# Mixture-of-experts routing by a gathered token list, with one shared-expert step after the expert tiles, in an eight-layer kernel on one core

## The reference, cut to what matters

```
def _L2_ffn_ref(x, router_w, expert_bias, w1, w3, w2, sw1, sw3, sw2):
    E, NSH, TOPK = (8, 2, 2)                      # HID = 256
    def _ffn(x, w1, w2, w3):
        return jax.nn.silu(x @ w1.T) * (x @ w3.T) @ w2.T
    xf = x.reshape(-1, d)                          # the normalised x
    shared = jnp.zeros_like(xf)
    for i in range(sw1.shape[0]):                  # two shared experts, every token
        shared = shared + _ffn(xf, sw1[i], sw2[i], sw3[i])
    logits = xf @ router_w.T + expert_bias
    rw, sel = jax.lax.top_k(logits, TOPK)          # each token's two best of 8 experts
    rw = jax.nn.softmax(rw, axis=-1)
    combine = jnp.einsum('tk,tke->te', rw, jax.nn.one_hot(sel, E))
    # out = sum over the 8 experts of combine[:, e] * _ffn(xf, w1[e], w2[e], w3[e])
    return out + shared
x = x + _L2_ffn_ref(_layernorm(x, axis=-1), ...)
x = x + _L3_xattn_ref(_layernorm(x, axis=-1), ctx_768, ...)
```

## Time and profile before

| | |
|---|---|
| median of 3 runs | 541.45 us (539.92 to 545.09) |
| the profiled execution's own time | 537.47 us |
| its span in the profile | 535.3 us, so 2.2 us lie around it |
| busy: PE, DVE, ACT, POOL | 84%, 71%, 51%, 35% |
| L2's mixture of experts in the span | from 359.7 us (first shared product) to 441.6 us (last tile's down product) |

### The profile page before, as it was taken

The page is one execution under the profiler, slowest core; times in us unless marked ns, Lnnn a source line. Parts: engine busy times, 40 slices in busy tenths (PEclk is TensorE's granted clock), DMA queues, the critical chain, the costliest instruction groups (busy, mean ns, idle before and its releaser), DMA issues.

```text
span 535.3 us, 9362 instructions
## 1 busy us (share of the span) xinstructions
PE 451.3 (84%) x3045; PEld 317.5 (59%) x3045; DVE 378.2 (71%) x1371; ACT 271.2 (51%) x854; POOL 189.7 (35%) x220
## 2 busy tenths in 40 slices
PE   3940689999988999999878989999989987777976
PEld 2310689899553567667446546775656653654845
DVE  4799988936766467863696868875744476938776
ACT  2798487620515566653245526652233348547553
POOL 5999994030231900001401553026420515110042
PEclk9755579999999999999999999999999998879999
DMA  7107000000455000000001230000341211000001
GB/s 259 78 1 299 6 2 3 1 1 1 157 222 239 0 3 1 2 1 1 1 12 28 67 85 1 2 1 29 101 118 40 70 45 46 10 1 1 1 0 39
DMA packets 17846, 26.46 MB, mean 49 GB/s; under 512 B 1988, under 2 KB 15236, under 8 KB 17287
## 3 DMA queue, kind: packets, MB, share of 16 engines
q1 hardware_dynamic: 16774, 23.78, 12.9%
q0 software_dynamic: 1024, 2.10, 1.4%
HBM read 21.07 MB, written 6.77 MB: 52 GB/s over the span
## 4 chain that ended last, share of the span: by engine, by line
PE 57%; DVE 19%; POOL 11%; ACT 6%; issue 5%; DMA 1%; SPq 0%; ACTq 0%; DVEq 0%; POOLq 0%
PE bank L1988 4%; PE bank L1054 3%; PE bank L791 3%; PE bank L1100 3%; PE bank L1081 3%; ACT arenaB L2405 3%; PE bank L2003 2%; PE bank L2349 2%; PE bank L2323 2%; PE bank L269 2%; PE bank L705 2%; PE bank L1724 2%; DVE arenaB L439 2%; PE bank L1697 2%; PE bank L262 2%
## 5 line engine op out<-in xcount | busy, mean ns | idle before, releaser
L218 POOL TENSOR_SCALAR rtmp<-mv 128x4 f32<-128x4 f32 x14 | 3.5, 248 | 130.6 <-DVE mv L197 106.4
L269 PE MATMUL bank<-in_ctx 128*128 128x512 f32 (+2 forms) x124 | 38.6, 439 | 0.0
L2405 ACT ACTIVATE arenaB<-bank,arenaB 128x77 f32<-128x77 f32 x88 | 27.2, 353 | 10.8 <-DVE arenaB L2424 10.7
L1988 PE MATMUL bank<-arenaA,in_dft 128*128 x60 | 30.6, 594 | 1.9 <-issue 1.9
L1111 DVE TENSOR_REDUCE nmax<-bank 128x1 f32<-128x512 f32 x32 | 20.5, 684 | 13.2 <-PE bank L1054 13.2
L2323 PE MATMUL bank<-arenaB,xnT 128*128 128x385 f32 (+1 forms) x48 | 22.5, 605 | 7.3 <-ACT arenaB L2405 6.7
L2048 ACT ACTIVATE in_dft<-bank 128x256 f32<-128x256 f32 x30 | 11.5, 384 | 33.7 <-PE bank L1988 33.7
L2215 DVE TENSOR_TENSOR in_ffn<-in_dft,bank 128x256 f32<-128x256 f32 x30 | 12.6, 419 | 22.3 <-ACT in_dft L2048 22.3
L439 DVE MATCH_REPLACE8 arenaB<-arenaB 128x77 f32<-128x77 f32 x128 | 26.8, 223 | 0.0
L269 PEld LDWEIGHTS bank<-in_ctx 128*128 128x128 f32 x124 | 19.4, 191 | 12.3 <-issue 11.7
L276 ACT COPY xnT<-bank 128x512 f32<-128x512 f32 x14 | 8.2, 585 | 34.8 <-PE bank L262 34.8
(11 more groups left out here) (511 smaller groups left out, 1358.8 us busy)
## 6 DMA issues: line engine op xcount, KB each, us to landing
arenaA<-in_moe_dram SPq DMA_DIRECT2D x1, 3840.0 KB, 11.7
in_dft<-in_dft_dram SPq DMA_DIRECT2D x1, 2048.0 KB, 7.5
in_dft<-in_head_dram SPq DMA_DIRECT2D x1, 2048.0 KB, 7.4
arenaA<-in_l_dram SPq DMA_DIRECT2D x1, 2048.0 KB, 16.0
xs_scratch<-in_moe_dram SPq DMA_DIRECT2D x2, 960.0 KB
arenaB<-xs_scratch SPq DMA_DIRECT2D x6, 256.0 KB, 3.4
ys_scratch<-arenaB SPq DMA_DIRECT2D x6, 256.0 KB
vw_scratch<-in_dft SPq DMA_DIRECT2D x32, 38.5 KB
```

The costliest lines, as they stand in the source:

```text
L269: nc.tensor.matmul(bank[into][:, 0:width], ident, packed["ctx"][:, 0:width], start=True, stop=True)
L1988: nc.tensor.matmul(bank[i % 2][:], xsT[:, g % 2, (i - i0) * P:(i - i0 + 1) * P], V["moe"][:, bass.ds(off[i], 2 * HE)], start=True, stop=Tr ...
L2405: ins = nc.scalar.activation(p3[:, n % 3, h, :], bank3(n, i)[:, (h - h0) * NC:(h - h0 + 1) * NC], ACT.Exp, bias=mx3[:, n % 3, h:h + 1], ac ...
```

## The change

Four things are done together.

1. *The list is made on chip the other way round.* `vec_route_slots` also builds, from each token's slot, two sets of 0/1 (or token-number) matrices, and `pe_inverse` multiplies them: 8 matmuls give, for each tile and each place in it, the number of the token that belongs there (0 for padding). DVE copies it to `token` (`vec_tokens`).
2. *Rows are gathered, not scattered.* SP stores the normalised rows in order to `xn_scratch` (256 KB for each batch). POOL issues one indirect gather for each of the 15 tiles from `xn_scratch` straight into `xs` on chip. The scatter, its waits, SP's reloads and the filling of `xs_scratch` near the start are gone. The tile groups become (0,3), (3,7), (7,11), (11,15).
3. *One shared step is moved.* `NSTEP` is 6: step 3 (expert 9, batch 1) leaves the half-steps. Its two up half-steps stand on PE behind tiles 28 and 29 (`i >= NT2`), its down product in `pe_attend3` between `scores(1)` and `scores(2)`, its addition to `X` on DVE at n = 1 of `vec_attend3`.
4. *Orders around it.* Batch 1's scores, places and slots move to n = 4, 4 and 5; `pe_offsets(0)` from n = 7 to n = 4. Batch 0's transposes into L3 and ACT's `warm` now stand behind the moved step.

```
-TILE_GROUPS = [(4 * g, min(4 * g + 4, TILES)) for g in range(-(-TILES // 4))]
+TILE_GROUPS = [(max(4 * g - 1, 0), 4 * g + 3) for g in range(-(-TILES // 4))]
...
-            sp.wait_ge(bias_rows, 48)
-            for b in range(NB):
-                sp.dma_start(A[f"xs_scratch{b}"].rearrange("(p j) d -> p (j d)", p=P), A["moe"][:, 0:TILES * D]).then_inc(bias_rows, 16)
...
-        NSTEP = 2 * len(SHARED)
+        NSTEP = 2 * (len(SHARED) - 1)
...
+        def pe_inverse(pe, b):
+            pe.wait_ge(*past(inverse_ready, b + 1))
+            for g in range(2 * TB):
+                ins = nc.tensor.matmul(bank[6 + b][:, P:P + TILES], at_place[:, g, :], in_tile[:, g, :], start=(g == 0), stop=(g == 2 * TB - 1))
+            ins.then_inc(inverse_mm[0], 1)
...
         def pe_moe(pe):
...
                 if n == 3:
-                    pe_turn(pe, ln_done, NT * 8, xn, [1], TURN8)
+                    pe_inverse(pe, 0)
                 if n == 4:
                     pe_logits(pe, 1)
-                if n == 7:
-                    pe_rank(pe, 1)
+                    off.extend(pe_offsets(pe, 0))
                 if n < NSTEP:
...
+                    pe_shared_up(n)
-                if n == NSTEP - 1:
-                    off.extend(pe_offsets(pe, 0))
+                if n == 3:
+                    pe_turn(pe, ln_done, NT * 8, xn, [1], TURN8)
+                if n == 5:
+                    pe_rank(pe, 1)
                 if n == NSTEP + 1:
                     pe_turn_tiles(pe, 0)
...
         def pe_tiles(pe, off):
...
+                    if i == 0:
+                        pe_inverse(pe, 1)
...
-                if i == NT2:
-                    pe_turn(pe, ln_done, NT * 9, xn, [0], TURN3)
+                if i >= NT2:
+                    pe_shared_up(NSTEP + i - NT2)
+            pe_turn(pe, ln_done, NT * 9, xn, [0], TURN3)
...
         def act_tiles(act):
...
                 if i == NT2:
-                    nc.scalar.activation(warm[:], ident[0:1, 0:1], ACT.Exp)
-                    act_turned(act, 7, which=[0], banks=TURN3)
+                    act_shared(act, NSTEP)
                 if i - 2 in LAST2:
                     act_ys(act, LAST2[i - 2])
+            act_shared(act, NSTEP + 1)
+            nc.scalar.activation(warm[:], ident[0:1, 0:1], ACT.Exp)
+            act_turned(act, 7, which=[0], banks=TURN3)
...
+        def pool_rows(pool, b):
+            pool.wait_ge(*past(token_ready, b + 1))
+            pool.wait_ge(*past(xn_stored[b], 16))
+            for g, (i0, i1) in enumerate(TILE_GROUPS):
+                if b:
+                    pool.wait_ge(xs_in[g], 16 * (i1 - i0))
+                for i in range(i0, i1):
+                    nc.gpsimd.indirect_dma_start(out=xs[:, b * TILES + i, :], out_offset=None, in_=A[f"xn_scratch{b}"],
+                                                 in_offset=bass.IndirectOffsetOnAxis(ap=token[:, b, i:i + 1], axis=0)).then_inc(xs_in[g], 16)
...
         def sync_tiles(sp):
...
+            for b in range(NB):
+                sp.wait_ge(ln_done, NT * 8 + (b + 1) * TB)
+                sp.dma_start(A[f"xn_scratch{b}"].rearrange("(q p) d -> p q d", p=P), xn[:, b * TB:(b + 1) * TB, :]).then_inc(xn_stored[b][0], 16)
...
         def vec_route_slots(dve, st, b):
...
             st.link(Vv.tensor_reduce(slotf, rks, AX.X, ALU.add))
-            Vv.tensor_scalar(slot[:, b, :], slotf, float(P), None, ALU.mult).then_inc(slot_ready[0], 1)
+            st.link(Vv.tensor_scalar(tmag, slotf, -63.5 / P, MAGIC, ALU.add, ALU.add))
+            st.link(Vv.scalar_tensor_tensor(below_tile, tmag, MAGIC, slotf, ALU.subtract, ALU.subtract))
+            if b:
+                dve.wait_ge(*past(inverse_mm, b))
+            Vv.tensor_tensor(at_place, bm(V["place"], 2 * TB), bc(below_tile, P, 2 * TB, P), ALU.is_equal)
+            st.link(Vv.tensor_tensor(in_tile, bm(V["jmag"], 2 * TB), bc(tmag, P, 2 * TB, TILES), ALU.is_equal))
+            Vv.tensor_tensor(in_tile, in_tile, bc(V["token"], P, 2 * TB, TILES), ALU.mult).then_inc(inverse_ready[0], 1)
+            Vv.tensor_scalar(slot[:, b, :], slotf, float(P), None, ALU.mult)
...
+        def vec_tokens(dve, b):
+            dve.wait_ge(*past(inverse_mm, b + 1))
+            nc.vector.tensor_copy(token[:, b, 0:TILES], bank[6 + b][:, P:P + TILES]).then_inc(token_ready[0], 1)
...
         def vec_moe(dve, st):
-            for n in range(NSTEP + 4):
-                if n == NSTEP - 1:
+            for n in range(NSTEP + 3):
+                if n == 4:
+                    vec_route_scores(dve, st, 1)
+                    vec_route_places(dve, st, 1)
+                if n == 5:
                     vec_route_slots(dve, st, 1)
                 if n < NSTEP:
+                    vec_shared(dve, n)
...
                 if n == 0:
                     vec_route_slots(dve, st, 0)
+                if n == 1:
                     vec_normalise(dve, 8, X, xn, [1])
-                if n == 4:
-                    vec_route_scores(dve, st, 1)
-                if n == 5:
-                    vec_route_places(dve, st, 1)
-                if n == 6:
+                    vec_tokens(dve, 0)
+                if n == 3:
                     vec_route_weights(dve, st, 0)
...
         def vec_tiles(dve, st):
...
+                if i == 0:
+                    vec_tokens(dve, 1)
+                if i == 6:
+                    vec_route_weights(dve, st, 1)
...
-                if i == NT2 - 1:
-                    vec_normalise(dve, 9, X, xn, [0])
+            vec_normalise(dve, 9, X, xn, [0])
+            vec_shared(dve, NSTEP)
+            vec_shared(dve, NSTEP + 1)
...
             scores(0)
+            pe.wait_ge(hid_ready, NSTEP + 2)
             scores(1)
+            pe.wait_ge(*past(ys_ready, NG2))
+            pe_shared_down(len(SHARED) - 1)
             scores(2)
```

More of the change, by code:

```diff
@@ L75 @@
     "l3f": [("wfcT", HID3), ("wpT", HID3)],
-    "rank": [("before", P), ("below8", NE * NE), ("jrow", TILES)],
+    "rank": [("before", P), ("below8", NE * NE), ("jrow", TILES), ("jmag", TILES), ("place", P), ("token", 2 * TB)],
 }
@@ L337, in tokens @@
             return v.rearrange("b (a g q) d -> g a b q d", a=LA, q=TB)[g]
-        scattered = [sem(f"scattered{b}") for b in range(NB)]
         def sync_loads(sp):
@@ L1870, in program @@
         rks = part(f0_flat, 552, 2 * TB, NE)
+        tmp2_flat = tmp2[:].rearrange("p t d -> p (t d)")
+        in_tile, tmag, below_tile = part(tmp2_flat, 0, 2 * TB, TILES), part(tmp2_flat, 120, 2 * TB), part(tmp2_flat, 128, 2 * TB)
+        at_place = part(arenaB, 5120, 2 * TB, P)
+        hid_last = part(tmp2_flat, 0, 2, S)
+        token = sb("token", P, NB, 16, dt=U32)
         slot, woff = sb("slot", P, NB, 2 * TB, dt=U32), sb("woff", 1, NB, 16, dt=I32)
@@ L1889, in program @@
         tile_hid, tile_hT = (sc_max, 4 * NT), (pT_dve, 2 * NT)
-        xs_in = [loaded["ctx"], loaded["rows"], loaded["s4"], loaded["dft"]]
+        wsum_mm, tern_ready = (ff_mm, NT), (skip_ready, NB)
+        inverse_mm, token_ready = (dft_mm, 5), (kern_pe, 4)
+        xn_stored = [loaded["ctx"], loaded["rows"]]
+        xs_in = [sem(f"xs_in{g}") for g in range(len(TILE_GROUPS))]
         ys_stored = loaded["ffn0"]
@@ L1927, in pe_turn_tiles, with pe_shared_up, pe_shared_down @@
             ins.then_inc(xs_turned[0], 1)
+        def pe_shared_up(n):
+            (e, b), c = SHARED[n // 2], n % 2
+            w = V["moe"][:, e * WE:(e + 1) * WE]
+            nc.tensor.matmul(bank[n % 2][:], w[:, c * P:(c + 1) * P], xnT[:, b * S:(b + 1) * S], start=True, stop=True).then_inc(up_mm, 1)
+            nc.tensor.matmul(bank[2 + n % 2][:], w[:, HE + c * P:HE + (c + 1) * P], xnT[:, b * S:(b + 1) * S],
+                             start=True, stop=True).then_inc(up_mm, 1)
+        def pe_shared_down(m):
+            e = SHARED[m][0]
+            w = V["moe"][:, e * WE:(e + 1) * WE]
+            hid = hid_last if m == len(SHARED) - 1 else hid2[:, m % 2]
+            for q4 in range(TB):
+                for c in range(2):
+                    ins = nc.tensor.matmul(bank[4 + m % 2][:, q4 * P:(q4 + 1) * P], hid[:, c, q4 * P:(q4 + 1) * P],
+                                           w[:, 2 * HE + c * P:2 * HE + (c + 1) * P], start=(c == 0), stop=(c == 1))
+            ins.then_inc(down_mm, 1)
         def pe_moe(pe):
```

109 lines of the change are left out of this document (45 added, 64 removed).

## The result

The changed kernel takes 547.88 us (median; 541.83 to 551.26), the kernel before 542.06 us (538.45 to 545.36) on the same chips, 20 runs each. The ratio is 1.0088, with an interval of 1.006 to 1.0115: slower by 0.9%. The ratio is formed from the fast runs and stands for 4.8 us; the plain medians are 5.8 us apart. Forecast were 548.0 us, 6.5 us more than before.

The account below looks back on a forecast made before the run. PE's instruction order was taken to bound the kernel wherever no other engine makes it wait. Front with second inverse +2.1, tail +4.7, L3 -0.3 sum to +6.5 us: 541.45 + 6.5 = 548.0 us, range 543 to 552.

Parts of the forecast that it names:

- The front: First slots to first tile: the 5.2 us taken out go into inverse, offsets and two waits; +0.45 us.
- the wait before down(2): Front: PE idle 3.1 us until DVE, behind all of batch 1's routing, makes half-step 5's product.
- The offsets: Front: reading batch 0's offsets at n = 4, with only the logits ahead, costs 1.3 us, bounds 0 and 2.1.
- rival D: Front: half clock after the idle before down(2), up to 1.7 us more, 549.7 us; counted within the forecast's 0.52.
- the gap of some 1 us behind the second logits: Front: sign that the forecast is right, PE waiting there for the reading of batch 0's offsets, priced at 1.3 us.
- The second inverse: In the PE-bound tiles (i = 0): batch 1's inverse matmuls add 1.65 us.
- The tail: Last tile to L3: moved up products, Silu and Exp's table load delay the first scores; +4.7 us, bounds 3.2 and 5.3.
- L3: Down(3) hidden in PE's idle between scores(1) and scores(2), shortening it; -0.3 us, bounds -3 and +1.5.
- A, level: Whole kernel: DVE's chain shorter, front PE-bound, L3 loses two half-clock stretches; -0.4 us, 541 us; chance 0.27.
- B, faster: Tiles' end: moved products fill PE's 2.4 us of idle; with other gains -5.9 us, 535.5 us; chance 0.10.
- C, gathers late: POOL: every gather takes 2.1 us plus 0.3, so batch 0's rows come late; about 556 us; chance 0.11.
- The filling of the scratch: Near the start, at 42.80 us, while the chain lay on POOL's arithmetic: its removal gives 0.

Follow-up runs that it names:

- r4: Changed kernel with DVE's product of half-step 5 ahead of batch 1's slots; ratio 1.001 to the kernel before.
- r6: Changed kernel with Exp's table loaded ahead of the moved step's activations, which are plain copies instead of Silu; tail 5.42 us.
- r7: Changed kernel with both orders changed: half-step 5's product ahead of batch 1's slots, and the copy to xnT ahead of up(7); ratio 1.002 to the kernel before.
- r9: r4 with the moved up products put into PE's idle time at the end of the tiles; ratio 0.9969 to the kernel before.
- r3: Changed kernel with the two scratch fills near the start put back, into memory nobody reads; ratio 1.0144 to the kernel before.
- r1: Changed kernel with only the shared step moved: scatter, filling and reload kept, no inverse or gathers; ratio 1.0047 to the kernel before.
- r11: r9's orders with rows scattered, filled and reloaded as before, without any inverse; ratio 0.9984 to the kernel before.
- r5: Changed kernel with L3's transposes and copy ahead of the last down product, up(7) and the last Silu; ratio 1.0068 to the kernel before.
- r2: Changed kernel with the gather alone, all eight shared half-steps ahead of the tiles; costs 0.99% against the kernel before.
- r10: r9 with batch 0's slots behind DVE's product of half-step 1 and its inverse behind up(3); ratio 0.9979 to the kernel before.

## Why the prediction was right

**The front** was forecast at +0.45 and came at +0.06. Step by step: the slots' wait 0.71 for 0.9, the inverse 1.81 for 1.65, `at_place` 1.22 for 1.2, the wait before down(2) 3.21 for 3.1 with the releaser that was named. Two terms do not hold. The offsets were priced at 1.3 us, by the idle at tile 8; they cost 0.1. And the half clock behind the wait, left to rival D, cost 0.76 us on down(2) and 0.84 more on the first tile, which the tiles' row holds.

The cheap offsets did not win 1.2 us by themselves, because DVE's chain decides when down(2) starts. They brought PE's rank forward, and with it DVE's slots, which in the forecast waited 0.9 us for it and here follow the addition at once (382.43). So down(2) starts 23.87 us after the first shared product (387.47 - 363.60), where the forecast has 24.92: 1.05 earlier. It then takes 2.55 us where the forecast has 1.9. The two errors are of opposite sign and nearly cancel; that the front came within 0.4 us is luck in part. Of the signs that the prediction named, the gap of some 1 us behind the second logits did not show. That DVE's order makes the wait is shown by r4: with one product moved the front fell from 26.42 to 22.30, and the ratio by 0.8%.

Why the offsets were mis-sized: the whole idle at tile 8 (1.94 us) was taken as the price of the reading. After the change the same place shows 1.00 us, and another releaser:

```profile
406.12 1.12 PE L2008 MATMUL bank<-arenaA,in_dft 128*128 x2 [1.00 <-DVE in_ffn L2260]
```

In all eleven changed kernels, the two that scatter among them, this gap is 0.97 to 1.07 us; 1.94 stands in the kernel before alone, and no run shows why. At n = 4, behind the logits' eight matmuls, the reading adds 0 to 0.24 us over all kernels whose clock was full there.

**The second inverse and the tiles**, forecast +1.65, came at +1.98. Made of rows: the inverse 1.87 us (391.72 to 393.59), the first tile's products 1.70 us at half clock (390.02 to 391.72) where r4 has 0.86 at full clock, so 0.84, less 0.94 for the shorter gap at tile 8: 1.77 of the 1.98. The forecast had the inverse alone, so here too two terms that it did not have nearly cancel. Front and tiles together make +2.04, forecast +2.1.

```profile
391.72 2.02 PE L1924 MATMUL bank<-tmp,arenaB 128*128 128x15 f32 x16
393.59 1.10 PE L2008 MATMUL bank<-arenaA,in_dft 128*128 x2
```

**The tail**, forecast +4.7, came at +4.55, and link by link in the rows: up(6) and tile 29's product 2.16 us (forecast 2.15), half of up(7) 1.06 (1.05), Silu 0.61 (0.6), table load and activation 1.41 (1.5). The chain is right, but the forecast's lower bound of 3.2 took the table load for a price that could be won back whole. It is not 1.5 in that sense: r6 takes it off the path and wins 0.7, since PE's transposes stand behind both moved products all the same. PE's order carries the other 3.9. The drain that the Trainium skill adds (ScalarE: Activation LUTs, section "What ACT_TABLE_LOAD costs") would by its figure have made an estimated +6.1; neither the row nor the sum has it.

**L3**, forecast -0.3, shows +0.49. Down(3) is hidden as expected, and the half clock behind the third scores is gone: from scores(0) to batch 1's transposes (L262) it is 27.85 us against 29.20. In r6 and r7 it is there again behind the same 1.34 us of idle, so the shorter idle does not always prevent it. What follows in the profile is 1.84 us longer, with the granted clock at 0.73 and 0.84 from 496 to 504 us, where before has 1.00. Over all kernels here the stretch from scores(0) to the end varies between 92.50 and 95.49 us, so neither number is a finding.

**The rivals.** *A, level*: false as the change stands, as DVE's chain was too long to hide, though 1.05 us shorter than put together. r4 takes that wait away and arrives at level, with 1.001. Its front and tiles stand 3.05 us under those of before, below the -2.3 that the forecast gave as its lower bound with the offsets at 1.3 us. *B, faster*: false, PE reaches up(6) only after its waits. r9 moves the products into them: against r4, tiles and tail fall from 61.0 to 58.5 us, where before has 55.5, so 2.5 of the 5.5 us come back, by PE's order and the earlier table load together. *C, gathers late*: false, with 0.96 us each. *D, half clock*: took place, 1.6 us on down(2) and the first tile where up to 1.7 was priced.

**The filling of the scratch**: no gain was forecast for its removal, and no profile shows one at the place; the time of r3 leaves that open by about half a per cent.

**Level of the time.** The forecast added 6.5 us to the median of before. The medians are 5.8 us apart, the two profiles 7.1 without what lies ahead of L2, and the ratio stands for 4.8; the forecast lies inside that spread. That 548.0 meets the median of 547.88 so closely is luck: the median of before moved by 0.6 us with more runs, and the terms missed by up to 1.2 us each.

## What to carry to other kernels

A step moved out of a front that is bound by PE gives back its PE time only if the other engines' chains get shorter too: here DVE's routing of batch 1, in one block ahead of a product that PE needs, took 3.2 us of the 5.2, and moving that one product ahead of the block was worth 0.8% of the time, half clock behind the wait included. Before moving work to an end of a stage "where PE has idle time", look on which side of the waits the moved instructions stand: behind them they cost in full, between them nearly half of it came back. And the inverse, eight small products per batch and 1.8 us each time on PE, costs about as much as the waiting for reloaded rows that it replaces (2.51 us in r1, 3.43 in r11, and half clock on down(2) behind it): with good orders the scatter (0.9984) and the gather (0.9969) can't be told apart.

## What was not expected of the hardware

The granted clock falls to 1.2 GHz behind short idle times of PE, but not each time, and for stretches of different length. The front is the same code in the changed kernel, r3, r5 and r6; it took 26.42, 29.25, 26.50 and 29.25 us. In the changed kernel down(2) took 2.55 us behind 3.21 us of idle, in r3 3.57 us behind 3.33. The wait of 0.71 or 0.72 us for the first inverse is in eight of the kernels. In r3, r6, r7 and r9 a stretch of 4 to 6 us mostly at half clock followed it, worth 1.7 us between r4's front and those of r7 and r9; in the changed kernel, r2, r4 and r5 none. In r10 two idle times of 0.97 and 0.96 us, 7 us apart, were followed by some 10 us mostly at half clock; the first of them, before the rank, is in every kernel here. In r2 the 1.80 us of idle before up(7) were followed by none. What decides between these, no run here separates. A single profile of this kernel therefore carries 3 us or more that belong to no edit, as at 74 and 268 us, and a wait of PE costs its own length and often something behind it: 3.21 us and 0.76 on the next product in this change.

The reading of 15 offsets into PE's registers shows 0.1 us behind eight small matmuls in the changed kernel and at most 0.24 in any, while PE is idle for 1.00 us at tile 8, and for 1.94 in the kernel before.
